# Two chunks of 512 tokens run as interleaved streams, with all three rotary operations of a tile on VectorE and all scaling of probabilities on GpSimd

## What is computed

```
xn  = layernorm(x)
out = x + attn(xn) + ffn(xn)
attn(x):  h = layernorm(x); q, k, v = projections, rotary on q and k   # 16 heads of 8, 4 key heads, window 32
          x = x + softmax(q k^T / sqrt(8)) v @ Wo
          return x + gelu(layernorm(x) @ Wf1) @ Wf2
ffn(x):   for l in range(2):
            h = shift_token(x)                # half of the channels comes from the token before
            q, k, v = h @ wqkv                # 8 heads of 64
            q, k = l2norm(q)*qs, l2norm(k)*ks; q, k = rotary(q, k)
            x = x + local_attention(q, k, v) @ wo       # query i sees keys i-64 .. i
            h = layernorm(shift_token(x)); a, g = h @ w1
            x = x + (a * gelu(g)) @ w2
```

## Time and profile before

| | |
|---|---|
| median of 3 runs | 1451.54 us (1446.1 to 1462.14) |
| the profiled execution | 1459.8 us, its span 1458.1 us |
| PE busy | 1124.0 us, 77% of the span |
| DVE busy | 878.6 us, 60% |
| ACT busy | 768.9 us, 53% |
| POOL busy | 291.5 us, 20% |
| mean granted PE clock | 0.877 |

### The profile page before, as it was taken

One profiled execution on the slowest core, in us unless ns is written; L12 is line 12 of the kernel. 1 busy time (PEld: TensorE's weight loads), 2 busy tenths in 40 slices (PEclk: granted clock), 3 DMA queues, 4 the chain that ended last, 5 costly groups with the idle time before them and its releaser, 6 DMA issues. The chain is left out here.

```text
span 1458.1 us, 23509 instructions
## 1 busy us (share of the span) xinstructions
PE 1124.0 (77%) x8682; PEld 620.1 (43%) x8754; DVE 878.6 (60%) x1738; ACT 768.9 (53%) x1928; POOL 291.5 (20%) x228
## 2 busy tenths in 40 slices
PE   5986788678698668867869877886787976797677
PEld 4752453154374245325437425432534732542353
DVE  5549655963445865596345596468545467648744
ACT  1355674485235556447523556653942453945574
POOL 1105112410101411241010141033202033204210
PEclk9698899889859879988986988997997796999799
DMA  6003101400101310140010131023001014003100
GB/s 260 1 29 117 27 1 58 112 2 15 31 1 45 101 27 1 58 112 2 15 32 1 51 98 23 1 73 98 2 15 32 1 59 111 2 1 123 48 16 15
DMA packets 39201, 66.22 MB, mean 45 GB/s; under 512 B 5408, under 2 KB 19232, under 8 KB 37152
## 3 DMA queue, kind: packets, MB, share of 16 engines
q1 hardware_dynamic: 37920, 62.43, 14.0%
q10 hardware_dynamic: 1152, 2.10, 0.4%
HBM read 13.12 MB, written 2.10 MB: 10 GB/s over the span
## 5 line engine op out<-in xcount | busy, mean ns | idle before, releaser
L494 POOL TENSOR_TENSOR qk<-pc,ps_ 128x512 f32<-128x512 f32 x128 | 194.3, 1518 | 583.8 <-DVE ps_ L1040 583.8
L872 ACT ACTIVATE prob<-bank,negb,inv_norm 128x128 f32<-128x128 f32 x512 | 233.0, 580 | 57.3 <-DVE negb L1087 57.3
L1040 DVE TENSOR_TENSOR ps_<-rot,tab_s 128x512 f32<-128x512 f32 x128 | 172.5, 1347 | 25.9 <-DMA rot<-raw 25.9
L872 ACT ACTIVATION_READ_ACCUMULATOR prob<-bank,negb,inv_norm 128x1 f32 x512 | 163.3, 328 | 0.0
L510 PE MATMUL bank<-hTz,wb_s 128*128 128x512 f32 x256 | 139.5, 675 | 4.3 <-ACT sq L980 4.3
L1085 DVE TENSOR_REDUCE negb<-bank 128x8 f32<-128x1024 f32 x64 | 78.3, 1223 | 94.5 <-PE bank L628 94.4
L976 ACT ACTIVATE raw<-bank,vec_s 128x512 f32<-128x512 f32 x128 | 90.0, 703 | 81.6 <-PE bank L510 46.5
L500 POOL TENSOR_TENSOR prob<-prob,recb 128x512 f32<-128x512 f32 x64 | 66.7, 1041 | 320.1 <-DVE recb L1107 320.1
L1038 DVE TENSOR_TENSOR pc<-raw,tab_s 128x512 f32<-128x512 f32 x128 | 109.3, 854 | 18.2 <-ACT raw L976 18.1
L656 PE MATMUL bank<-probT,vS 128*64 128x64 f32 x1024 | 67.9, 231 | 38.6 <-issue 34.2
L510 PE MATMUL bank<-hTz,w_s 128*128 128x512 f32 (+1 forms) x192 | 87.8, 602 | 12.2 <-DVE hTz L1127 12.2
(11 more groups left out here) (151 smaller groups left out, 2020.8 us busy)
## 6 DMA issues: line engine op xcount, KB each, us to landing
rot<-raw SPq DMA_DIRECT2D x256, 128.0 KB, 2.0
vS<-vB SPq DMA_DIRECT2D x24, 512.0 KB, 4.4
vS<-vB SPq DMA_DIRECT2D x8, 384.0 KB, 5.7
xn_tok<-x SPq DMA_DIRECT2D x5, 512.0 KB, 3.6
tab_s<-tabs SPq DMA_DIRECT2D x1, 2048.0 KB, 21.0
vS<-x SPq DMA_DIRECT2D x4, 512.0 KB, 3.7
out<-vS SPq DMA_DIRECT2D x8, 256.0 KB, 2.4
wb_s<-wb SPq DMA_DIRECT2D x1, 1536.0 KB, 16.6
```

Of the source, the lines that this page charges most:

```text
L494: pool.tensor_tensor(dst, pc[:, j % 2, :], ps_[:, j % 2, :], ALU.add).then_inc(sum_rdy, 1)
L872: ins = act.activation(prob[:, t % 2, g, h, :], s_bank[t % 2][:, g, h * P:(h + 1) * P], ACT.Exp, bias=negb[:, t % 2, g, h:h + 1], scale=qu ...
L1040: dve.tensor_tensor(ps_[:, j % 2, :], rot[:, jb % 4, :], st, ALU.mult).then_inc(prod_rdy, 1)
```

## The change

The two chunks become two streams, and every engine's program is written out anew so that they overlap:

- Layer by layer, the window attention of chunk 0 lies inside the projections of chunk 1, and the window attention of chunk 1 inside the head product, layer norm and gated hidden part of chunk 0. The remaining part of chunk 1 of layer 0 is mixed with the projections of chunk 0 of layer 1 and with the first branch's hidden part.
- The window attention goes by units of one group of one tile (8 units a chunk), in steps: step i has the scores, maxima and exponentials of unit i, the reciprocal of unit i-1, the turning and laying of unit i-2, and every second step a weighing. `AFTER_TILE` and `AFTER_VALUES` say after which tile or value product of chunk 1 a step of chunk 0 stands, on all engines alike.
- DVE adds `pc` and `ps_` itself. POOL scales the probabilities of both groups, and for this branch does nothing else.
- The ring has 3 banks and 3 `raw` and `rot` slots; the fourth bank holds the sums of squares, banks 4 to 7 two score banks, one for turning and one for heads.
- The copies of turned probabilities are all ACT's for chunk 0 and all DVE's for chunk 1 (`LAY_VECTOR`).
- The shifted values move tile by tile, for chunk 0 between the `rot` transfers of chunk 1.

```diff
-RING = 4
+RING = 3
+SIDE = 3
+SLOTS = 3
+
+AFTER_TILE = {3: (0,), 4: (1,), 5: (2, 3), 6: (4,), 7: (5,)}
+AFTER_VALUES = {0: (6,), 1: (7,), 2: (8,), 3: (9,)}
+LAY_VECTOR = ((False, False), (True, True))
...
+                    for n in range(LAYERS * TILES * 2):
+                        t, g = n // 2, n % 2
+                        pool.wait_ge(win_rec[g], t + 1)
+                        p = prob[:, n % 3, :, :]
+                        pool.tensor_tensor(p, p, wide(recb[:, t % 2, g, :]), ALU.mult).then_inc(win_norm[g], 1)
...
                     for l in range(LAYERS):
...
+                        for k in range(B_QK):
+                            project(l, 1, k)
+                            if k == 2:
+                                copy_norms(l, 0)
+                            for i in AFTER_TILE.get(k, ()):
+                                step(l, 0, i)
...
+                        for i in range(4):
+                            step(l, 1, i)
+                        centred(l, 0)
+                        step(l, 1, 4)
+                        step(l, 1, 5)
+                        log(l, 0)
+                        root(l, 0)
+                        step(l, 1, 6)
+                        step(l, 1, 7)
+                        gelus(l, 0)
...
+                            dve.tensor_tensor(pc[:, j % 2, :], raw[:, jb % SLOTS, :], ct, ALU.mult)
+                            dve.wait_ge(rot_rdy[jb % SLOTS], 32 * (jb // SLOTS + 1))
+                            dve.tensor_tensor(ps_[:, j % 2, :], rot[:, jb % SLOTS, :], st, ALU.mult)\
+                               .then_inc(prod_rdy, 1)
...
+                            dve.wait_ge(prod_rdy, jb + 1)
+                            dve.tensor_tensor(qk[:, qk_tile(k), cc(c)], pc[:, j % 2, :], ps_[:, j % 2, :],
+                                              ALU.add).then_inc(sum_rdy, 1)
...
+                        norms(l, 0)
+                        for k in range(B_QK):
+                            turn_pairs(l, 1, k)
+                            if k == 2:
+                                scale(l, 0, (0, 1))
+                            if k == 3:
+                                scale(l, 0, (2, 3))
+                            for i in AFTER_TILE.get(k, ()):
+                                step(l, 0, i)
```

More of the change, by code:

```diff
@@ L61 @@
 V_N = V_L + LAYERS * VL_N
[L65 to L75, removed]
@@ L166, in program @@
             pass
[L167 to L170, removed]
+        raw = sb("raw", [P, SLOTS, CH])
+        rot = sb("rot", [P, SLOTS, CH])
+        prob = sb("prob", [P, 3, 4, P])
+        probT = sb("probT", [P, 2, 4, P])
         sq = sb("sq", [P, 4, CH])
@@ L229, in program @@
         shift_rdy = sem("shifted")
+        edge_rdy = sem("edge_shifted")
         on_rdy = sem("heads_copied")
@@ new lines, in step, with centred @@
+                    def step(l, c, i):
+                        if i < 2 * TPC:
+                            window_probs(l, c, i)
+                        if 2 <= i < 2 * TPC + 2 and not LAY_VECTOR[c][i % 2]:
+                            lay(act, l, c, i - 2)
+                        if i >= 5 and i % 2:
+                            window_out(l, c * TPC + (i - 5) // 2)
+                    def centred(l, c):
+                        i = USE["ln", l, c]
+                        mid, square, _, _ = ln_buffers(l, c)
+                        act.wait_ge(mm_full, i + 1)
+                        act.activation(mid, bank[:, i % RING, :], ACT.Copy).then_inc(cen_rdy, 1)
+                        act.activation(square, bank[:, i % RING, :], ACT.Square).then_inc(drained[i % RING], 1)
@@ L1016, in _ @@
+                    a_hidden(1, 0)
+                    a_hidden(1, 1)
+                    centred(1, 1)
+                    a_hidden(1, 2)
+                    a_hidden(1, 3)
+                    log(1, 1)
+                    root(1, 1)
+                    gelus(1, 1)
                 @block.vector
@@ new lines, in scale, with turn_pairs @@
+                    def scale(l, c, tiles):
+                        for k in tiles:
+                            i = USE["norm", l, c, k]
+                            dve.wait_ge(sum_rdy, pair(l, c, k) + 1)
+                            dve.wait_ge(mm_full, i + 1)
+                            z = qk[:, qk_tile(k), cc(c)]
+                            dve.tensor_tensor(z, bank[:, i % RING, :], z, ALU.mult).then_inc(drained[i % RING], 1)
+                    def turn_pairs(l, c, k):
+                        r = 2 if k < 4 else 0
+                        rotate(l, c, k, USE["qk", l, c, k], tab_s[:, r, cc(c)], tab_s[:, r + 1, cc(c)])
```

967 lines of the change are left out of this document (510 added, 457 removed).

## The result

| | before | after |
|---|---|---|
| median, lowest to highest (us) | 1450.22, 1446.1 to 1462.14 | 1691.07, 1685.16 to 1694.87 |
| ratio after to before | | 1.164, 95% interval 1.157 to 1.172 |
| profiled span, granted clock of PE | 1458.1, 0.877 | 1689.4, 0.807 |
| busy PE / DVE / ACT / POOL | 1124.0 / 878.6 / 768.9 / 291.5 | 1299.1 / 832.6 / 792.6 / 163.4 |

The change made the kernel slower by 241 us, where the forecast had 124 (1575, range 1495 to 1645). The sign and the closed chain were right; the loss is nearly twice the forecast. Some executions of a kernel run in a slower state of the chip, and medians and ratios here leave them out: two of e5's four and one of e7's four, the traced one. The page of the changed kernel has these rows: busy times, then the granted clock of PE in 40 slices.

What follows compares the result with a forecast made beforehand. No engine bounds all stages: DVE bounds projections, ACT window attention, PE the MLP. Twice +36.5, -23, -17 and -2 make +31 a sequence, +124 in all, so 1584 profiled and about 1575 us, range 1495 to 1645.

Steps and rivals of the forecast that it cites:

- the closed chain: Chunk 1's projections from tile 3: maxima, exponentials, `raw` copy, exchange and rotary operations wait in turn, 7.4 us a tile.
- The second chunk's scores start at 63.7: Chunk 1's first `ps_` to second chunk's scores: 63.7 us where 27.2 before, +36.5 a layer.
- the stage from those scores to layer 1: Second chunk's scores to layer 1's first chunk 1 `ps_`: 27 less by the walk, 23 less with the clock.
- start to chunk 1's first `ps_`: Start of a sequence: 2 us less, from a shorter `rot` wait; chunk 0 gives less than it loses waiting for the root.
- scores to the end: End of a sequence, behind layer 1's second chunk scores: 76 us with 4 for the clock, before 93.0, 17 less.
- the middle turn: Chunk 1's projections, tile 5 to tile 6: two units and two `probT` copies ahead, 10.1 us.
- I add 4, a guess between 0 and 12: Stage from chunk 1's scores to layer 1: 4 us added for PE's low clock, making 27 less into 23 less.
- Rival 1: PE stays at 1.2 GHz through the second chunk's stages: +12 in place of +4, 1640 us and beyond; chance 0.10.
- sequence at 392 us: Sign expected in the changed kernel's profile: one whole sequence takes 392 us.
- Rival 2: POOL's scalings meet the rotary operations, five a layer at 1.04 us each: +42, 1617 us; chance 0.07.
- Rival 3: Chain not closed, chunk 1's stretch set by DVE's work: 36 us instead of 63.7, total of 1355 us; chance 0.08.
- Rival 4: Chain holds, but the walk through other stages misses 30 us a sequence of PE and ACT overlap: 1450 us; chance 0.05.

Runs made afterwards that it cites:

- e5: Changed kernel without the exchange of rows, `ps_` computed from `raw` (partner rows missing from the rotation): 1554.7 us.
- e7: Changed kernel with product and copies one tile ahead and chunk 0's turned probabilities copied by DVE instead of ACT: 1546.8 us.
- e10: Changed kernel with chunk 0's turned probabilities copied by DVE instead of ACT, nothing else: 1646.2 us.
- e14: Changed kernel with ACT's copy of the head bank ahead of the exponentials in odd window steps: 1668.7 us.
- e6: Kernel before with the rotary addition on DVE and chunk 0's shifted value copies issued tile by tile between chunk 1's exchanges: 1443.0 us.
- e1: Changed kernel with PE's product and ACT's two copies of tile k+1 ahead of the window steps after tile k (k = 3 to 6): 1573.1 us.
- e9: Kernel before with the rotary addition on DVE and both chunks' shifted value copies issued behind chunk 1's last exchange: 1425.0 us.
- e4: Kernel before with only the rotary addition moved from POOL to DVE: 1443.2 us.
- e2: Changed kernel with all of chunk 0's window steps behind chunk 1's projections and values instead of among them: 1659.4 us.

## Why the prediction was right in direction and wrong in size

Right were the sign and the closed chain. **What failed is the size of the chain's term:** "The second chunk's scores start at 63.7" measured 72.4 in layer 0 and 70.7 in layer 1, so that the stretch grew by 45.3 and 43.6 and not by 36.5. Next to it, the stage from those scores to layer 1 was walked at 86.1 and took 92.4.

Per sequence, means of the four (the last has no end of its own). The forecast is given as the level that the prediction named.

| term | before: sequence used, mean | forecast | after, mean | step's error |
|---|---|---|---|---|
| start to chunk 1's first `ps_` | 109.1, 105.3 | 2 less: 103.3 | 102.3 | -1.0 |
| chunk 1 stretch, layer 0 | 27.2, 27.1 | 63.7 | 72.4 | +8.7 |
| scores to layer 1's chunk 1 | 109.1, 107.5 | 86.1 | 92.4 | +6.3 |
| chunk 1 stretch, layer 1 | 27.2, 27.1 | 63.7 | 70.7 | +7.0 |
| scores to the end | 93.0, 92.0 | 76 | 78.1 | +2.1 |

- **The chain.** Right in mechanism: `ps_` is 0.69, and the simple turn measured 7.84 (forecast 7.4, and 7.9 with a copy: 7.84). The wait was foretold as one of 4 to 5 us ahead of `ps_`; it stands in two parts, 2.6 to 4.0 ahead of `pc` for ACT's copy and 1.8 to 2.6 ahead of `ps_`. Mis-sized were the turns with more in them: tile 4 at 19.5 (17.3), the middle turn 11.69 (10.1), tile 7 to the scores 25.7 (21). The walk let each engine have what it needed when its own list came to it, and did not ask what frees the one turning and the one head bank. e10 brings the middle turn to 10.3, e14 the last part to 22.7. Of the 2.2 at tile 4, 1.2 stand at tiles 1 and 2: each waits 0.5 for an exchange, as the same tiles do in e6, where two value issues stand between the exchanges, and comes 2.56 behind the one before instead of 1.95. The other 1.0 is the first scores, which ran at the lower clock (1.97):

```profile
547.72 0.69 DVE L1162 TENSOR_TENSOR ps_<-rot,tab_s 128x512 f32<-128x512 f32 x1 [0.53 <-DMA rot<-raw]
...
558.69 0.69 DVE L1213 TENSOR_REDUCE negb<-bank 128x4 f32<-128x512 f32 x1 [2.67 <-PE bank L650]
```

- **"I add 4, a guess between 0 and 12"** for the clock. Rival 1 described the mechanism (PE carries the lower clock out of the first chunk's stages), and the changed kernel's own execution shows its price at the entry. The stage from the scores to layer 1 took 92.4, 93.9 and 93.0 where the first scores took 1.97, and 90.3 where the clock rose within them (1.66); layer 1's took 80.1 against 77.1 and 77.0. So the entry alone is worth 2 to 4 a stage, about the guess; even with all of the +6.3 on top of that guess the stage stays below the rival's +12. The measured time lies in the rival's range because the other terms were short as well. What the +6.3 is made of, no run shows.
- **The sample.** "The four sequences repeat one another, so the sum is made for one" does not hold: the sequence chosen took 365.6, the mean is 359.0. The start was forecast as a change, so its base drops out; the other terms were walked as levels and compared with a base 2.8 too long, 11 us in four sequences. The "sequence at 392 us" does not follow from the sum either, which gives 365.6 + 31 = 396.6; measured were 415.9.
- **Rival 2** (scalings meeting rotary operations) did not occur in the changed kernel, but does in e1. **Rival 3** fell: the chain is closed, and even opened (e1) the stretch takes 56.9 and not the 36 that DVE's work alone would give. **Rival 4** fell too: the walk through the other stages was not too long but too short.

Counted over four sequences the stretches are 63 us, the stage from the scores to layer 1 is 25, the end 8, the sample 11 and the start -4: 103 or 104 of the 107 us between the forecast's 124 and the 231 of the two profiled spans. The range was too narrow at its upper end because the walks had no queueing behind shared banks and no exchange behind an issue, so that all errors but the start's had one sign.

## To carry to other kernels

When two streams are interleaved by hand, look for the producer of the next piece on each in-order engine: one step of a consumer stream ahead of it on two engines closes a loop (here 7.84 a tile, where the three rotary operations take 1.95), and moving that producer one step ahead took 118 us off here. Ask of every buffer that became single which copy frees it and what stands ahead of that copy; and take the base of a sum from all repetitions of a loop, not from one. A small transfer that an engine waits for shortly should stand ahead of large ones that are needed late (e9 against e4, 18 us), and issues themselves take room on a queue (0.59 and 0.60 each in e6).

## What the runs showed of the hardware that was not expected

- **The clock follows a wait into the next stage.** e2's window units had 0.50 for 40.07 us although PE was busy in 32.90 of them. The same list of instructions took 90.3 or 92.4 to 93.9 in the changed kernel, 89.5 or 94.4 in e10, by the clock at which PE entered it (above). In e1's execution the same start of a sequence (to the first `ps_`, 72.20 us) was complete in 72.2 in the third sequence at a granted clock of 0.86, and took 78.5 in the second, whose first 72.2 us had 0.77. The two matmuls of a projection tile took 1.92 in the changed kernel at 578.13 (above).

```profile
415.47:487.67 72.20, 65.02 (x617) 46.68 (x618) 38.04 (x68) 28.10 (x51) 5.18 (x4) 0.77 0.03 9
804.48:876.68 72.20, 65.80 (x630) 45.43 (x630) 38.83 (x69) 33.13 (x61) 5.19 (x4) 0.86 0.04 14
```

- **Half an array costs the time of a whole one.** 16 matmuls in two of the quarters took 1.09, 32 in all four 1.10. The Trainium skill (TensorEngine Tiling (Array Packing), "Key Properties") says that different tiles can load and multiply in parallel; the two times agree with that. With the groups split PE's time for the scores doubled, 86.5 to 179.8 us (the mean granted clock was lower as well, 0.807 instead of 0.877).
- **An exchange of 128 rows in two transfers takes nearly the same time wherever it stands.** With nothing ahead of it, and the copy finished just before `pc`, the wait behind `pc` was 1.79 to 1.87 (before, after, e6, e9, e10); with large value transfers ahead it was 4.09 and 5.17. Tile 6 of layer 0 in the changed kernel is an exception that was not explained (2.63 to 3.29).
